# Packed block and expert numbers: one register load per group and per part

## What is computed

```python
z = h @ W_func.T                                        # gnn
e = leaky_relu(concat([z[src], z[dst], w]) @ W_att.T)
alpha = softmax of e over the edges of one destination
agg = segment_sum(alpha[:, None] * z[src], dst)
h_new = relu(where(deg > 0, h @ W_self.T + agg, h)); return h + h_new
# mix: linear attention of 8 heads, layernorm, 256-1024-256 relu network, layernorm
# ffn: a router picks 2 of 6 experts per row; each expert is a 256-256-256-256 network
top_w, top_i = top_k(softmax(router(features)), 2)
out = sum over the two of softmax(top_w) * expert[top_i](features)
```

## Time and profile before

| | us |
|---|---|
| median of 3 runs | 2349.81 (2349.37 to 2350.4) |
| profiled execution | 2345.32 |
| its span | 2343.3 |
| mean granted TensorE clock | 0.879 |
| busy: PE / DVE / POOL / ACT | 1930.4 / 1649.2 / 1465.6 / 687.6 |

### The profile page before, as it was taken

One profiled execution on the slowest core, in us unless ns is written; L12 is line 12 of the kernel. 1 busy time (PEld: TensorE's weight loads), 2 busy tenths in 40 slices (PEclk: granted clock), 3 DMA queues, 4 the chain that ended last, 5 costly groups with the idle time before them and its releaser, 6 DMA issues.

```text
span 2343.3 us, 43283 instructions
## 1 busy us (share of the span) xinstructions
PE 1930.4 (82%) x11471; PEld 1505.6 (64%) x11471; DVE 1649.2 (70%) x4135; ACT 687.6 (29%) x2860; POOL 1465.6 (63%) x1188
## 2 busy tenths in 40 slices
PE   6999699678888888888888888888867778899991
PEld 5555688556666666666666656666644458788881
DVE  6997699977777767777666766776756656445564
ACT  2444688531111111111111111111102344444550
POOL 5000556677888888888888788888780153744366
PEclk9999555579899999998898988889998789999996
DMA  8887888544445544445544444445557754545464
GB/s 216 260 256 226 280 284 295 160 126 121 123 123 132 154 124 124 123 125 146 138 123 122 124 123 122 122 123 138 138 124 182 171 154 113 154 136 145 138 171 124
DMA packets 308206, 368.12 MB, mean 157 GB/s; under 512 B 118624, under 2 KB 261707, under 8 KB 304982
## 3 DMA queue, kind: packets, MB, share of 16 engines
q1 hardware_dynamic: 165292, 223.65, 32.0%
q0 software_dynamic: 135840, 136.92, 24.4%
q10 hardware_dynamic: 6975, 6.40, 0.9%
HBM read 279.68 MB, written 85.98 MB: 156 GB/s over the span
## 4 chain that ended last, share of the span: by engine, by line
PE 40%; issue 13%; DVE 11%; DMA 7%; DVEq 4%; POOL 3%; SPq 2%; ACT 1%; ACTq 0%; POOLq 0%
PE bank L677 39%; DMA wexp<-func_rows,a_src 5%; DVE acc L1823 4%; DVEq L1580 2%; POOL wexp L641 2%; DVE onehot L1810 1%; DMA g_all<-sorted_d 1%; SPq L369 1%; POOL g_all L664 1%; PE bank L1026 1%; DVE work L1596 1%; DVEq L1823 1%; DVE work L1599 1%; DMA work<-mix_rows 0%; PE bank L849 0%
## 5 line engine op out<-in xcount | busy, mean ns | idle before, releaser
L641 POOL DMA_INDIRECT wexp<-func_rows,a_src x850 | 1060.9, 1248 | 263.4 <-issue 193.7
L677 PE MATMUL bank<-wexp,onehot 125*125 125x257 f32 x1700 | 557.2, 432 | 215.6 <-DVE acc L1823 156.1
L1823 DVE TENSOR_TENSOR acc<-bank,acc 125x257 f32 x850 | 355.7, 419 | 381.0 <-PE bank L677 244.4
L677 PEld LDWEIGHTS bank<-wexp,onehot 125*125 125x125 f32 x1700 | 316.8, 206 | 391.9 <-issue 298.2
L1810 DVE TENSOR_SCALAR onehot<-iota_r,a_rel,a_hi 125x125 f32<-125x125 f32 x850 | 320.7, 380 | 0.1
L609 POOL TENSOR_TENSOR work<-iota_h,a_hi 125x500 f32<-125x500 f32 x85 | 109.2, 1286 | 246.9 <-PE bank L714 165.4
L677 PE MATMUL bank<-g_all 128*128 128x128 f32 x1840 | 230.0, 278 | 15.4 <-issue 6.1
L654 POOL DMA_INDIRECT sorted_d<-acc,work x100 | 122.4, 1224 | 180.9 <-DVE acc L1967 98.0
L677 PEld LDWEIGHTS bank<-g_all 128*128 128x128 f32 x1840 | 217.8, 194 | 19.0 <-ACT g_all L1301 7.4
L664 POOL DMA_INDIRECT g_all<-y_d,work x100 | 131.0, 1310 | 139.2 <-DVE g_all L2137 77.8
L677 PE MATMUL bank<-w_s,work 128*125 128x256 f32 x800 | 216.2, 419 | 0.0
(11 more groups left out here) (275 smaller groups left out, 2817.4 us busy)
## 6 DMA issues: line engine op xcount, KB each, us to landing
wexp<-lr_d SPq DMA_DIRECT2D x85, 625.0 KB
wexp<-in_attr SPq DMA_DIRECT2D x25, 896.0 KB
sorted_d<-spare SPq DMA_DIRECT2D x72, 256.0 KB, 4.8
g_all<-sorted_d SPq DMA_DIRECT2D x115, 128.0 KB
y_d<-g_all SPq DMA_DIRECT2D x115, 128.0 KB, 3.1
wexp<-func_rows,a_src POOLq DMA_INDIRECT x850, 4.0
work<-xn_rows SPq DMA_DIRECT2D x38, 224.0 KB
xnT_d<-work SPq DMA_DIRECT2D x25, 250.0 KB, 4.4
```

The costliest lines, as they stand in the source:

```text
L641: pool.indirect_dma_start(ring[:, z, 0:D], None, func_rows, bass.IndirectOffsetOnAxis(ap=a_src[:, n // CS, n % CS:n % CS + 1], axis=0)).th ...
L677: return pe.matmul(o, l, r, start=first, stop=last_, **kw)
L1823: v.tensor_tensor(to, bank[3 + z % 2][0:R, 0:D + 1], to, ALU.add).then_inc(s("summed"), 1)
```

## The change

Four block numbers (below 64) are packed into one word and seven expert numbers (below 8) into another; registers hold the packed words, and each use takes its number out by shift and mask. A group loads 9 words once, instead of 17 numbers twice. A part of the tiles loads 7 words once per engine instead of eight numbers at a time. VectorE packs the block numbers in the first pass (`pack_blocks`, at g = 20), in floating point, and the expert numbers in `route_slots`.

```diff
-SUBS = ((0, 17), (17, ZS))
-IDS = 8
+PACK = 9
+EPACK = 7
...
-        iota_t = sb("iota_t", [1, 48])
+        iota_t = sb("iota_t", [1, EPACK * EPACK])
+        powers = sb("powers", [1, EPACK, EPACK])
+        blk_pk = sb("blk_pk", [1, GROUPS * PACK], I32)
-        te_i = per[0:1, 850:850 + ALL_TILES].bitcast(I32)
+        te_i = per[0:1, 850:850 + len(PARTS) * EPACK].bitcast(I32)
+        te_p = per[0:1, 900:900 + EPACK]
-        te_f = sb("te_f", [1, max(TILES)])
+        te_f = sb("te_f", [1, EPACK * EPACK])
...
             def choose(k):
                 p = TPART[k]
-                if k not in experts:
+                if p not in experts:
                     pe.wait_ge(s("slots"), p + 1)
-                    n = min(IDS, TILE0[p] + TILES[p] - k)
-                    _, values = nc.values_load_multi_w_load_instructions(
-                        te_i[:, k:k + n], engines=[mybir.EngineType.PE], min_val=0, max_val=EXPERTS - 1,
...
-                    for a in range(n):
-                        experts[k + a] = values[a]
-                return bass.ds(experts[k], 1)
+                    _, experts[p] = nc.values_load_multi_w_load_instructions(
+                        te_i[:, p * EPACK:(p + 1) * EPACK], engines=[mybir.EngineType.PE], min_val=0, max_val=(1 << 24) - 1,
...
+                z = k - TILE0[p]
+                return bass.ds(((experts[p][z % EPACK] >> (3 * (z // EPACK))) & 7).with_bounds(min_val=0, max_val=EXPERTS - 1), 1)
```

`act_expert` and `picked_expert` are changed in the same way. On VectorE:

```diff
+            def pack_blocks():
+                v.wait_ge(s("blk_in"), 16)
+                t.settle()
+                t.did(v.tensor_copy(blk_f, blk_row[:]))
+                t.settle()
+                each = blk_f.rearrange("p (g z) -> p g z", z=ZS)
+                to = blk_s.rearrange("p (g z) -> p g z", z=PACK)
+                t.did(v.scalar_tensor_tensor(to, each[:, :, PACK:2 * PACK], 64.0, each[:, :, 0:PACK], ALU.mult, ALU.add))
+                t.settle()
+                t.did(v.scalar_tensor_tensor(to, each[:, :, 2 * PACK:3 * PACK], 4096.0, to, ALU.mult, ALU.add))
+                t.settle()
+                n = ZS - 3 * PACK
+                t.did(v.scalar_tensor_tensor(to[:, :, 0:n], each[:, :, 3 * PACK:ZS], 262144.0, to[:, :, 0:n], ALU.mult, ALU.add))
+                t.settle()
+                t.did(v.tensor_copy(blk_pk[:], blk_s))
+                t.settle()
+            for q in range(EPACK):
+                t.did(v.memset(powers[:, q, :], float(8 ** q)))
...
+                if g == 20:
+                    pack_blocks()
...
-            def blocks_of(n, count):
+            def blocks_of(i):
                 _, values = nc.values_load_multi_w_load_instructions(
-                    blk_row[:, bass.ds(n, count)], engines=[mybir.EngineType.DVE], min_val=0, max_val=BLOCKS - 1,
+                    blk_pk[:, bass.ds(i * PACK, PACK)], engines=[mybir.EngineType.DVE], min_val=0, max_val=(1 << 24) - 1,
...
-                return values
+                return [((values[z % PACK] >> (6 * (z // PACK))) & 63).with_bounds(min_val=0, max_val=BLOCKS - 1) for z in range(ZS)]
...
-                at = sub(i, 0)
+                at = blocks_of(i)
...
-                steps(i, at, 15, 17)
-                at = sub(i, 1)
-                steps(i, at, 17, 19)
+                steps(i, at, 15, 19)
...
-                o.did(v.tensor_scalar(te_f[:, 0:TILES[p]], iota_t[:, 0:TILES[p]], r_e[0:1, 2, 0:1], None, ALU.is_ge))
+                o.did(v.tensor_scalar(te_f[:], iota_t[:], r_e[0:1, 2, 0:1], None, ALU.is_ge))
...
             def route_slots(p):
...
+                o.did(v.tensor_tensor(te_f[:], te_f[:], powers[:].rearrange("p q m -> p (q m)"), ALU.mult))
                 o.settle()
...
-                o.did(v.tensor_copy(te_i[:, TILE0[p]:TILE0[p] + TILES[p]], te_f[:, 0:TILES[p]]))
+                o.did(v.tensor_reduce(te_p, te_f[:].rearrange("p (q m) -> p m q", q=EPACK), AX.X, ALU.add))
+                o.settle()
+                o.did(v.tensor_copy(te_i[:, p * EPACK:(p + 1) * EPACK], te_p))
```

More of the change, by code:

```diff
@@ L309, in build @@
         onehot = sb("onehot", [R, AHEAD, R], stack=place)
+        blk_f = onehot[0:1].rearrange("p a b -> p (a b)")[:, LROW:LROW + STEPS]
+        blk_s = onehot[0:1].rearrange("p a b -> p (a b)")[:, 0:GROUPS * PACK]
         junk = onehot[:].rearrange("p a b -> p (a b)")[:, 0:LROW]
@@ L573, in _ @@
             pool.memset(ones_row[:], 1.0).then_inc(s("consts"), 1)
-            pool.iota(iota_t[:], [[1, 48]], base=0, channel_multiplier=0, **iota).then_inc(s("consts"), 1)
+            pool.iota(iota_t[:], [[1, EPACK * EPACK]], base=0, channel_multiplier=0, **iota).then_inc(s("consts"), 1)
             own.did(pool.memset(ident[:], 0.0))
@@ L1010, in choose @@
                 p = TPART[k]
-                if k not in experts:
+                if p not in experts:
                     pe.wait_ge(s("slots"), p + 1)
-                    n = min(IDS, TILE0[p] + TILES[p] - k)
-                    _, values = nc.values_load_multi_w_load_instructions(
-                        te_i[:, k:k + n], engines=[mybir.EngineType.PE], min_val=0, max_val=EXPERTS - 1,
-                        skip_runtime_bounds_check_because="a count of five comparisons at most")
-                    for a in range(n):
-                        experts[k + a] = values[a]
-                return bass.ds(experts[k], 1)
+                    _, experts[p] = nc.values_load_multi_w_load_instructions(
+                        te_i[:, p * EPACK:(p + 1) * EPACK], engines=[mybir.EngineType.PE], min_val=0, max_val=(1 << 24) - 1,
+                        skip_runtime_bounds_check_because="seven counts of five comparisons each, packed by route_slots")
+                z = k - TILE0[p]
+                return bass.ds(((experts[p][z % EPACK] >> (3 * (z // EPACK))) & 7).with_bounds(min_val=0, max_val=EXPERTS - 1), 1)
             def tile_turn(k):
@@ L1318, in act_expert @@
                 p = TPART[k]
-                if k not in chosen:
+                if p not in chosen:
                     act.wait_ge(s("slots"), p + 1)
[L1321 to L1327, removed]
+                    _, chosen[p] = nc.values_load_multi_w_load_instructions(
+                        te_i[:, p * EPACK:(p + 1) * EPACK], engines=[mybir.EngineType.Activation], min_val=0, max_val=(1 << 24) - 1,
+                        skip_runtime_bounds_check_because="seven counts of five comparisons each, packed by route_slots")
+                z = k - TILE0[p]
+                return bass.ds(((chosen[p][z % EPACK] >> (3 * (z // EPACK))) & 7).with_bounds(min_val=0, max_val=EXPERTS - 1), 1)
             for i in range(-3, ALL_TILES):
@@ L1577, in _ @@
             v.wait_ge(s("selected"), QS)
-            def blocks_of(n, count):
+            def blocks_of(i):
                 _, values = nc.values_load_multi_w_load_instructions(
-                    blk_row[:, bass.ds(n, count)], engines=[mybir.EngineType.DVE], min_val=0, max_val=BLOCKS - 1,
-                    skip_runtime_bounds_check_because="tab_i is clamped to BLOCKS - 1 and counts up from 0")
-                return values
+                    blk_pk[:, bass.ds(i * PACK, PACK)], engines=[mybir.EngineType.DVE], min_val=0, max_val=(1 << 24) - 1,
+                    skip_runtime_bounds_check_because="four numbers below 64 each, packed by pack_blocks")
+                return [((values[z % PACK] >> (6 * (z // PACK))) & 63).with_bounds(min_val=0, max_val=BLOCKS - 1) for z in range(ZS)]
             def spread_of(own, z, st_, j):
@@ L1810, in one_hot @@
                 v.tensor_scalar(onehot[:, z % AHEAD, :], iota_r[:], at(a_rel), at(a_p), ALU.is_equal, ALU.mult).then_inc(s("onehot"), 1)
-            def sub(i, h):
-                z0, z1 = SUBS[h]
-                return dict(zip(range(z0, z1), blocks_of(i * ZS + z0, z1 - z0)))
             def steps(i, at, z0, z1):
@@ L1884, in body @@
                     mean_var(mid, st, mv, "var")
-                steps(i, at, 22, 23)
-                steps(i, at, 23, 24)
+                steps(i, at, 22, 24)
                 m_down(i)
@@ L2069, in route_tiles @@
                 for e in range(1, EXPERTS - 1):
-                    o.did(v.scalar_tensor_tensor(te_f[:, 0:TILES[p]], iota_t[:, 0:TILES[p]], r_e[0:1, 2, e:e + 1],
-                                                 te_f[:, 0:TILES[p]], ALU.is_ge, ALU.add))
+                    o.did(v.scalar_tensor_tensor(te_f[:], iota_t[:], r_e[0:1, 2, e:e + 1], te_f[:], ALU.is_ge, ALU.add))
                     o.settle()
@@ L2109, in picked_expert @@
                 p = TPART[k]
[L2110 to L2117, removed]
+                if p not in picked:
+                    _, picked[p] = nc.values_load_multi_w_load_instructions(
+                        te_i[:, p * EPACK:(p + 1) * EPACK], engines=[mybir.EngineType.DVE], min_val=0, max_val=(1 << 24) - 1,
+                        skip_runtime_bounds_check_because="seven counts of five comparisons each, packed by route_slots")
+                z = k - TILE0[p]
```

(1 more changed line is left out.)

## The result

The changed kernel took 2332.35 us at the median of 12 runs (2322.82 to 2340.65), beside 2345.06 us for 12 runs of the kernel before: a ratio of **0.9952, 95% interval 0.9936 to 0.9968**. The forecast was 2324 us in a range of 2312 to 2338, and a gain of 25.6 us; measured were 11 to 13.

A forecast was written before the change was run, and what follows sets the result against it. POOL's row gathers were taken to bound the loop at 52.3 us per group, PE the first pass and tiles. Terms summed to -25.6 us: 2345.3 to 2319.7 profiled, 2324 us as median; range 2312 to 2338.

The forecast's parts named there:

- (a): First pass: packing the block numbers takes 2.4 us, covered by PE's gapless stream: 0, bounds 0 and +2.4.
- (b): Loop: shift and mask on VectorE's queue, 0.15 us per step, hidden behind POOL's pace: 0.
- (c): Start of the loop: the second load goes, so POOL's wait for the full ring mostly goes: -2.5 us.
- (d): End of the loop: the last group's second load goes, decoding costs 1 us: -0.6 us, bounds -3.3 and +1.2.
- (e): route_slots: a product over 49 numbers and a reduction added for part 0: +0.5 us, bounds 0 and +1.
- (f): Tiles of part 0: four reloads disappear, decoding is covered by PE: -18.5 us, bounds -18.5 and -12.
- (g): Seam from part 0 to part 1: one load stays, that of one number goes: -1.0 us, bounds -4.7 and 0.
- (h): Tiles of part 1: less than half of the 8.0 us over PE's pace goes: -3.5 us; part 2: 0.
- I sum against the profiled execution and add the same 4.5 us: Whole kernel: terms are summed on the profiled execution, then 4.5 us added because the runs' median stood that much higher.
- R2: Loop: decoding on VectorE's queue becomes the limit, from 0.23 us per step on: +32 us, 2382 us, chance 0.04.
- R4: Loop: POOL's gathers get longer as VectorE holds POOL more often: +6 us, 2355 us, chance 0.03.
- R3: Tiles: part 0's gain meets POOL still scattering, first combination up to 12 us late: 2336 us, chance 0.14.

The follow-up runs named there:

- the second profile of the change: The changed kernel measured again with no edit, against the kernel before: 2317.86 us, 0.9916.
- the second and third measurement: The changed kernel measured twice more with no edit, against the kernel before: 2317.86 us, 0.9916, and 2318.29 us, 0.9905.
- the aligned rows above: The change with each row of packed words starting at a multiple of four words, against the kernel before: 2316.31 us, 0.9897.

## Why the prediction was right, and where not

Terms by the second profile of the change against the earlier trace rows and the windows above.

- (a) Right. The first addition came at 494.7 to 497.3 us in the profiles of the change, 495.9 before.
- (b) Right. The two operations stand behind the wait, at 0.15 us; the pace went from 49.3 to 50.1 us (50.0 in the second profile), under POOL's 52.3. That it is cover and not cheapness is shown by eight more operations, which cost 135 us.
- (c), (d) -3.1 forecast. From the first gather to the last addition it was 1335.7 us before and 1333.1, 1326.7 and 1332.0 in the three profiles of the change. Right, with a scatter as large as the term. At the start POOL's three stops, 4.5 us, have become one of 1.60 - 0.30 = 1.3 us.
- (e) Right: from the four comparisons that make `te_f` to the last copy, the end of the routing took 2.4 us before and 2.8 after, +0.4 where +0.5 was forecast.
- (f) -18.5 forecast, 105.09 to 88.65 = -16.4 measured.
- (g) -1.0 forecast, -1.6 measured. (h) -3.5 forecast, 155.14 to 152.13 = -3.0; part 2 went up by 1.1, forecast 0.

Tiles together: -23 forecast, 366.4 to 345.7 = -20.7. The rest of that profile's 28.0 us: 1.1 before the first gather, 2.6 in the loop, 0.2 after the tiles, and 3.4 in norm and router, which the change hardly touches: from the last addition of the loop to tile 0 it was 146.4 us before, 143.0 in this one, and 142.1 to 147.6 over all others.

**What failed.** The step "I sum against the profiled execution and add the same 4.5 us": the three runs shown stood high. Twelve runs of the kernel before had a median of 2345.06 us, so 4.5 us were no property of the kernel. And that 2332.35 us fell within the range is in part luck: the base that was 4.7 us too high made up for a part of the 13 us of gain that the first measurement didn't show. By its gain the mechanism is confirmed only by the second and third measurement. Of the forecast's 25.6 us, the first measurement shows 11 to 13, the next two 21.5 and 23.2. The profile behind the first had late semaphore steps and a tile stage 17.5 us longer; that the other eleven runs had some of them too is likely from their spread, but not shown, and what causes the lateness is open.

The rivals. R2's point of decision, "from 0.23 us per step on", was too low: at 0.29 us the groups went at 51.3. Between 0.29 us (51.3) and 0.70 us (57.5) POOL's 52.3 lies at about 0.36. The estimate had put the loads' whole 4.9 us and all of decoding on the chain. For the change's own two operations that fits (49.3 - 4.9 + 5.1 = 49.5 against 50.1 measured, and the aligned rows above); for further ones it doesn't, since they cost 0.6 us per group each where the queue has 2.4. Why the further ones hide and the first two don't isn't shown.

R4: a gather took 1250 ns instead of 1248, so nothing doubled. But the argument against R4, that the median is the minimum, was void: it says only that most gathers aren't held. Before the change 90 of 850 took over 1.26 us, and 72 of them ran beside a VectorE tensor-tensor operation with no input in PSUM, as this one of 1.55 us:

```profile
849.97 0.69 DVE L1599 TENSOR_TENSOR work<-work,rv 125x512 f32<-125x512 f32 x1
850.19 1.55 POOL L641 DMA_INDIRECT wexp<-func_rows,a_src  x1 [0.30 <-PE bank L677]
```

The 212 gathers with such a neighbour averaged 1351 ns, the other 638 averaged 1214; of the 31.5 us over 1211 ns each, 29.6 us belong to the 212 (32.2 of 33.4 us in the second profile of the change). The Trainium skill ("SBUF — State Buffer", SBUF: two separate sides) has VectorE operations with two SBUF inputs and GpSimd operations that read SBUF lock each other out of a shared port pair, a condition that the prediction left out; these rows agree with it. No run took such an operation away, so it is a coincidence in time, 34% of these gathers held against 3% of the others, and not a test. With the change it didn't grow: VectorE has the same operations before and after, and gathers took 1245 to 1254 ns on average whether the loads of block numbers took 0.85 or 3.9 us (1237 with eight more register operations).

R3: POOL's 7.47 us of idle time before its first gather back went to 0.31, as R3 had it, but that gather began at 2056.3 us instead of 2074.0, VectorE waited for no gathered rows in early part 1, and part 1 got no longer; so nothing was handed on. R1 and R5 fell.

**What was overlooked.** The prediction used alignment to price the loads but didn't ask what alignment alone would do. Here it does more than the change, with no decoding and no packing. Nor did it ask what holds a tenth of the gathers: those 31 us stand in the loop that POOL paces, and no run here tried to take them away.

## What to carry to other kernels

Before a load is made rarer, look at why single ones of its kind are three times faster: here the first word's place decided it, and moving the rows was worth more (0.987 and 0.986) than packing them (0.991). A cost that a slower engine covers is free up to that engine's pace and is paid beyond it, so count the pace of both, not the operations. Measure the base with as many runs as the result; and where a profile has waits for a releaser that it can't name, take a second one before explaining them.

## What the runs showed of the hardware

The times of register loads are as if four numbers went at a time when the first word is a multiple of four, and single ones otherwise. Aligned: 17 numbers 1.36 us, 9 numbers 0.85, 8 numbers 0.62, 7 numbers 1.06. Not aligned: 17 numbers 3.89 us, 9 numbers 2.07, 8 numbers 1.93. One number costs 0.23 us, and a group of four 0.28 to 0.31 ((1.36 - 0.23)/4 = 0.28; 0.62/2 = 0.31; by these seven numbers would take 0.31 + 3 x 0.23 = 1.00, measured 1.06). Hence seven aligned words cost more than eight, and a start that is off by two words is as slow as one off by one (the 12 loads of 17 numbers that start so before took 3.8 to 4.0 us): a load of 17 never gets back into step. The Trainium skill ("Runtime: NRT & Kernel Launch", Instruction fetch mechanics) gives about 200 ns per register even in bulk, for loads from HBM. These loads come from SBUF; unaligned they agree with it (229 ns), aligned they don't (80 ns), and the measurement decides.

A further register operation stands 0.07 us behind the one before on VectorE's queue. Beyond the change's own two, the first two further ones behind the wait cost 0.6 us per group of 34 each (18 ns per step), the next six 1.0 us each ((57.5 - 51.3)/6; 30 ns). The rest of their time doesn't show in the pace.

Before the change, POOL's row gathers took 1.35 us on average beside a VectorE tensor-tensor operation without an input in PSUM, and 1.21 us otherwise.
